# Both heads' masks at the start of a pair of steps: VectorE's order in an attention and mixture-of-experts kernel

## The reference

```python
xn = layernorm(x)                                   # x: 32 samples of 256 rows of 128
# attention: 16 heads of 64, rotary on the first 32 dims of Q and K
scores = where(causal, -inf, einsum('bhqd,bhkd->bhqk', Q, K)) / 8
attn = softmax(scores);  out = einsum('bhqk,bhkd->bhqd', attn, V) @ W_o
# mixture of experts: 8 experts of 128x512 and 512x128, and one "skip" choice
probs = softmax(xn @ router_w + router_b);  gates = the two largest of 9
moe = sum over e of gates[e] * (gelu(xn @ w1[e]) @ w2[e]) + gates[8] * xn
result = x + attention + moe
```

## Time and profile before

| | |
|---|---|
| median of 3 runs | 1558.59 us (1558.15 to 1562.15) |
| the profiled execution | 1554.54 us, span 1552.7 us |
| TensorE, busy share of the span | 81% |
| VectorE | 78% |
| ScalarE | 73% |
| GpSimd | 52% |
| mean granted TensorE clock | 0.947 |

### The profile page before, as it was taken

One profiled execution on the slowest core, in us unless ns is written; L12 is line 12 of the kernel. 1 busy time (PEld: TensorE's weight loads), 2 busy tenths in 40 slices (PEclk: granted clock), 3 DMA queues, 4 the chain that ended last, 5 costly groups with the idle time before them and its releaser, 6 DMA issues.

```text
span 1552.7 us, 47377 instructions
## 1 busy us (share of the span) xinstructions
PE 1263.4 (81%) x15156; PEld 982.4 (63%) x15157; DVE 1213.7 (78%) x4592; ACT 1134.4 (73%) x3606; POOL 806.5 (52%) x1324
## 2 busy tenths in 40 slices
PE   2415888888888888887899999788888888888887
PEld 2403666666666666665798988566666666666666
DVE  6788777777778777775677777788888888887885
ACT  6415777777777777776588887777877777777776
POOL 3243666666666666665000000466766766666665
PEclk9757999999999999999899999999999999999999
DMA  9522322222222222224122322333333333333330
GB/s 296 183 52 52 79 73 70 71 69 69 70 71 69 70 71 70 69 71 133 52 84 85 88 83 79 77 77 78 76 79 76 86 91 83 81 90 95 79 76 26
DMA packets 115839, 130.19 MB, mean 84 GB/s; under 512 B 11568, under 2 KB 75312, under 8 KB 115376
## 3 DMA queue, kind: packets, MB, share of 16 engines
q1 hardware_dynamic: 107056, 110.26, 28.2%
q0 software_dynamic: 8576, 17.33, 3.9%
HBM read 28.85 MB, written 31.59 MB: 39 GB/s over the span
## 4 chain that ended last, share of the span: by engine, by line
PE 42%; DVE 26%; issue 8%; DMA 5%; POOL 4%; ACT 2%; DVEq 0%; POOLq 0%; ACTq 0%
PE bank L1118 8%; DVE arena L972 8%; PE bank L1189 7%; PE bank L1119 7%; PE bank L1120 7%; DVE arena L934 5%; DMA stage<-sorted_y_dram,rows_at 4%; PE bank L1225 4%; PE bank L1199 4%; DVE arena L945 3%; DVE o_whole L1005 2%; DVE arena L933 2%; PE bank L1209 2%; PE bank L1226 1%; DVE stage L891 1%
## 5 line engine op out<-in xcount | busy, mean ns | idle before, releaser
L643 ACT ACTIVATE probs<-arena,neg_max 128x128 f32<-128x128 f32 (+1 forms) x1024 | 453.3, 446 | 109.6 <-DVE neg_max L972 102.5
L972 DVE CUSTOM_DVE_ANT_0 arena<-bank,causal 128x128 f32<-128x128 f32 (+1 forms) x1024 | 314.8, 344 | 2.7 <-PE bank L1189 2.7
L1189 PE MATMUL bank<-arena 64*128 64x128 f16 (+1 forms) x3072 | 179.4, 252 | 128.8 <-DVE neg_max L972 128.3
L501 POOL DMA_INDIRECT stage<-sorted_y_dram,rows_at x128 | 126.3, 986 | 260.9 <-DMA sorted_y_dram<-stage 238.4
L1199 PE MATMUL bank<-ident,probs 128*128 128x128 f32 x1536 | 241.9, 274 | 5.7 <-ACT probsT L626 5.5
L1189 PEld LDWEIGHTS bank<-arena 64*128 64x128 f16 x3072 | 102.9, 97 | 182.8 <-DVE neg_max L972 128.5
L1199 PEld LDWEIGHTS bank<-ident,probs 128*128 128x128 f32 x1536 | 183.2, 142 | 35.7 <-issue 6.4
L626 ACT ACTIVATE probsT<-bank 128x384 f32<-128x384 f32 x384 | 185.9, 484 | 19.3 <-PE bank L1199 19.2
L643 ACT ACTIVATION_READ_ACCUMULATOR probs<-arena,neg_max 128x1 f32 x1024 | 195.4, 191 | 0.0
L1225 PE MATMUL bank<-probsT,arena 128*64 128x256 f32 x1024 | 187.6, 425 | 0.9 <-ACT probsT L626 0.9
L1118 PE MATMUL bank<-xnT_lo,wqk_hi 128*128 128x256 f16 x512 | 143.4, 280 | 54.9 <-DVE arena L934 50.8
(11 more groups left out here) (155 smaller groups left out, 3430.0 us busy)
## 6 DMA issues: line engine op xcount, KB each, us to landing
arena<-arena SPq DMA_DIRECT2D x256, 256.0 KB, 4.7
arena<-sorted_x_dram SPq DMA_DIRECT2D x72, 128.0 KB, 2.1
sorted_y_dram<-stage SPq DMA_DIRECT2D x72, 128.0 KB, 1.8
sorted_x_dram<-arena SPq DMA_DIRECT2D x3, 2304.0 KB, 16.7
arena<-experts_dram SPq DMA_DIRECT2D x8, 512.0 KB, 5.1
out_dram<-acc SPq DMA_DIRECT2D x32, 128.0 KB
sorted_x_dram<-arena SPq DMA_DIRECT2D x1, 2368.0 KB, 16.2
sorted_x_dram<-stage,rows_at POOLq DMA_INDIRECT x128, 2.3
```

The source lines that it names most:

```text
L501: nc.gpsimd.indirect_dma_start(out=stage[:, k % BACKS, :], out_offset=None, in_=sorted_y[0:ROWS, :], in_offset=bass.IndirectOffsetOnAxis(a ...
L643: last = nc.scalar.activation(probs[:, s % 4, at:at + w], masked[:, s % 4, at:at + w], ACT.Exp, bias=neg_max[:, s % 4, t:t + 1], scale=-1. ...
L972: last = nc.vector.tensor_tensor_reduce(out=masked[:, s % 4, at:at + w], in0=SC[s % 2][:, at:at + w], in1=causal[:, at:at + w], scale=1.0, ...
L1189: last = mm(SC[h][:, at:at + w], q_stack[parity][rows, r, ql, u, qs], k_stack[parity][rows, r, kl, u, 0:w], start=(n == 0), stop=(n == 2))
```

## The change

VectorE's `mask` of one head becomes `masks` of two: at the even step it waits for the scores of the pair and for the exponentials of the heads up to s-3 (a wait that `invert` made before), masks head s and head s+1, and then inverts and splits the inverse. The rest of the even step and the rest of the odd step follow as they were. GpSimd waits for `cleared` before its first sample.

```diff
+            pool.wait_ge(cleared, 16 * 5)
             former_samples(sample)
...
-            def mask(b, s, at_fill):
-
-                if s % 2 == 0:
-                    dve.wait_ge(s_ready, 8 * b + s // 2 + 1)
-                    if not (at_fill and s < INV_LAG):
-
-                        invert(8 * b + (s - INV_LAG) // 2, (s - INV_LAG) % H // 2)
-                for t, (at, w) in enumerate(((0, P), (P, 2 * P))):
-                    last = nc.vector.tensor_tensor_reduce(
-                        out=masked[:, s % 4, at:at + w], in0=SC[s % 2][:, at:at + w], in1=causal[:, at:at + w],
-                        scale=1.0, scalar=MASKED, op0=ALU.add, op1=ALU.min, accum_out=neg_max[:, s % 4, t:t + 1])
-                last.then_inc(s_masked, 1)
-                if s % 2 == 0 and not (at_fill and s < INV_LAG):
+            def masks(b, s, at_fill):
+
+                dve.wait_ge(s_ready, 8 * b + s // 2 + 1)
+                if not (b == 0 and s < 4):
+                    dve.wait_ge(exp_done, 16 * b + s - 2)
+                for i in range(2):
+                    for t, (at, w) in enumerate(((0, P), (P, 2 * P))):
+                        last = nc.vector.tensor_tensor_reduce(
+                            out=masked[:, (s + i) % 4, at:at + w], in0=SC[i][:, at:at + w], in1=causal[:, at:at + w],
+                            scale=1.0, scalar=MASKED, op0=ALU.add, op1=ALU.min, accum_out=neg_max[:, (s + i) % 4, t:t + 1])
+                    last.then_inc(s_masked, 1)
+                if not (at_fill and s < INV_LAG):
+                    invert(8 * b + (s - INV_LAG) // 2, (s - INV_LAG) % H // 2)
                     split_inverse(8 * b + (s - INV_LAG) // 2, (s - INV_LAG) % H // 2)
...
             def sample(b, parity, at):
                 for s in range(H):
                     G = 16 * b + s
-                    mask(b, s, at in FILLS)
+                    if s % 2 == 0:
+                        masks(b, s, at in FILLS)
```

## The result

The changed kernel is slower. Its median over 4 runs is 1584.97 us (1569.44 to 1590.52), that of the kernel before beside it 1558.37 us: a ratio of 1.0146, 95% interval 1.01 to 1.0192. The forecast was 1530.6 us and a range of 1516 to 1560.

What follows compares the result with a forecast made beforehand. Waits, not a busy engine, were taken to bound the kernel, chiefly TensorE's scores waiting for mask maxima. First half -36, second half +9, odd samples -1 gave -28 us: 1526.5 profiled, 1530.6 us median, range 1516 to 1560.

Steps and rivals of the forecast that it cites:

- The loop of steps 2 to 8: Masks through turn, rope unit and transposes to next masks: 4.68 us a pair, 5.16 at step 4; no gain against now.
- The scores' wait: TensorE's scores waiting for the masks' maxima, 55.6 us in the first half, would fall to near zero.
- the rope unit's: TensorE's rope unit waiting for the turn: from 21.2 us in the first half to some 45.
- the attention product waits: On TensorE, a wait for the scaled output would appear, about 1 us per sample.
- GpSimd's wait for the clearing: Counted at nothing: it stands where GpSimd idles 25.67 us for the dispatch in any case.
- The rival of the clock that still falls: Gaps of 1.3 and 1.0 us around step 8 still lower the clock: 1545.6 us; chance 0.09.
- the masks of step 2 follow at once, as the scores no longer wait: First half: step 2's masks start when VectorE ends the pair of step 0, at 390.34.
- the term of 1.4 us: First half: step 10's attention product starts at 409.2 instead of 410.63, 1.4 us gained per sample.
- The 1.0 of the clock: First half, behind step 8's gap: the clock stays high, so about 1.0 us per sample comes back.
- the price of the second half: Later masks of step 10 delay gathers and a combine: +0.6 us per sample, +9 us over 15 samples.
- the rival of the gathers: Gathers become the second half's wait: 2.5 us lost per sample instead of 0.6, 1559 us; chance 0.12.
- The contention with GpSimd: VectorE's cast of the inverse waits for GpSimd's subtraction, 0.4 us four times a sample: 1579 us; chance 0.08.

Runs made afterwards that it cites:

- e5_mix_late: `e4_split_first` with VectorE's mix of the former sample moved from step 0 to step 10 in the first half: 1551.37 us, ratio 0.9942 to the kernel before.
- e7_no_clear_wait: The changed kernel without GpSimd's wait for the cleared rows: 1581.94 us, ratio 1.0161 to the kernel before.
- e4_split_first: The changed kernel with GpSimd's waits moved behind its split and rope addition, just ahead of the send or gather needing them: 1562.43 us, ratio 0.9984.
- e6_combine_behind: The changed kernel with the combines of steps 9, 11 and 13 moved one step on, behind the next masks: 1557.64 us, ratio 0.9996.
- e3_turn_ahead: The changed kernel with the odd mask directly behind the turn and the inversion ahead of the even mask: 1576.08 us, ratio 1.0094.
- e10_turn_three: The odd mask directly behind the turn, inversion ahead of the even mask, plus the edits of `e4_split_first`, `e5_mix_late` and `e6_combine_behind`: 1505.28 us, ratio 0.9657.

## Why the prediction was wrong

**What held.** The loop of steps 2 to 8 has the links that the forecast gave it: in the table 4.94, 5.42 and 4.79 for 4.68, 5.16 and 4.68, and in `e5_mix_late`, where nothing else disturbs it, 4.89, 5.22 and 4.75. The scores' wait went, the rope unit's rose to 46.1 and 44.9 us (some 45 forecast), the attention product waits 0.9 us a sample (about 1 forecast), and in the first half the gap of 2.90 us and the low clock behind it are gone: the granted clock of these 14 samples rose from 0.96 to 1.00. The four matmuls of step 10's attention product in sample 7 now take 0.66 us, not 1.13. That the change gains little or nothing in the loop was forecast too. GpSimd's wait for the clearing costs nothing that the runs can tell (`e7_no_clear_wait`). The rival of the clock that still falls is out for this profile.

**The first step that failed: "the masks of step 2 follow at once, as the scores no longer wait".** In sample 7 they come 0.90 us later than that (5.84 for 4.94). The forecast took VectorE's rows at the earlier trace rows as if their lengths and the supply of scores stayed the same. The forecast looked at what TensorE's scores had waited for, and not at what else they depend on once that wait is gone: the chain from a send that lands late, through GpSimd's split, ScalarE's copy and eviction, to the attention product. Of this, `e4_split_first` gives back 0.78 from step 0 to 2; the mix's slowness then costs it again, and only `e5_mix_late` has both off, at 4.07. In addition the links in sample 7 made 0.49 more than forecast over steps 2 to 8 (396.46, 401.80 and 406.55 for the later masks, so 15.01 for 14.52) and the last 0.05. Together 1.44: the attention product of step 10 starts 25.20 us after the sample's first scores (410.90 less 385.70), where it was 25.23 before (410.63 less 385.40) and 23.8 by the forecast. So the term of 1.4 us came out as nothing. The 1.0 of the clock came nearly whole: from that product to the next sample it was 12.47 and is 11.66, so 0.81.

**The second step that failed: the price of the second half, "+0.6 per sample", with ends of 0 and 1.3.** The mechanism was the right one, and the combines' delay was held to be one, at step 13. In the trace two combines wait, 1.72 us at step 9 and 2.23 at step 13, each directly ahead of a pair of masks, and what stands behind is not only the scores, but the exponentials and an eviction on which the next sample's start depends. The masks of step 2 in sample 20 start 5.30 us after the sample's first scores (1117.05 less 1111.75), where the forecast left them at 4.69 (1119.45 less 1114.76). `e6_combine_behind` takes 1.17 of the 1.32 away. The forecast followed the delay of the gathers as far as the next scores, and put it at 0.6; what it left out was what hangs on the exponentials and the eviction. This is the rival of the gathers in kind, given a chance of 0.12, at about half of its price (1.32 a sample against 2.5; the forecast itself had 0.6 of it).

**The rival that was put aside with a row.** The contention with GpSimd was given 0.08, for the four casts of the inverse, and for the two-input instruction it was held that the row of the low part at 406.84 does not show it. That reading was wrong: GpSimd was at work beside that row, and paid. Its first addition began 0.24 us behind the low part:

```profile
407.08 1.03 POOL L470 TENSOR_TENSOR arena<-arena 128x256 f32<-128x256 f32 x1 [0.87 <-DVE arena L934]
408.08 0.71 POOL L471 TENSOR_TENSOR arena<-arena 128x256 f32<-128x256 f32 x1
```

In the kernel before, 91 of the 128 first additions overlap a low part, and take 1.03 us on average; the other 37 take 0.73. The second addition bears on the gap of 2.90 us. The dispatch beside it (407.77) takes 1.10 us for two instructions, and the same two at step 0 take 0.59:

```profile
388.00 0.59 DVE L891 TENSOR_SCALAR stage<-acc,neg_mean,rstd 128x128 f32<-128x128 f32 x2
```

So some 0.5 us of that gap was contention already. In the changed kernel the mix is what suffers (12.9 us, and 8.4 in `e5_mix_late`, over 14 samples: 0.3 each, on the path at step 0), and in the second half the combine, which reads two SBUF tiles (6.9 us more over 14 samples; how much of it is on the path was not tried). In `e3_turn_ahead` it is the low part. The casts of the inverse went the other way, from 0.237 to 0.216 us (first half) and from 0.202 to 0.176 (second) on average of 112. So the mechanism was real and the place wrong.

**The sum.** By the profiled executions: first half -10.8 for 14 samples (forecast -33.6), second half +18.5 (forecast +8.4), and the rest +7.3 (forecast about -1, with the samples 15 and 31 each carrying a share of the halves' figures). In this rest are 2.1 us in sample 0, 2.8 in sample 15 with the experts, 3.1 in the last sample, 1.2 ahead of the first scores, and -1.8 in sample 16. These were not looked into.

**Open.** The median of the changed kernel lies 15.5 us above its profiled execution, that of the kernel before 3.8 above its own. Its runs spread from 1569 to 1591, at clocks of 0.970 to 0.957, and which samples are longer in the long ones no profile shows. The profile of `e7_no_clear_wait` (1576.23 us) has both halves longer by 0.2 a sample at the same mean clock of 0.970, so it is not the clock alone. The low clock in the opening and in the experts was not examined either.

## What to carry to other kernels

When a wait is taken away, follow back each thing that the freed instruction depends on, not only the one it was waiting for: the next latest may be a few tenths of a microsecond behind, and here it was a split on GpSimd that stood behind a transfer's landing. Put waits for transfers just ahead of the instruction that needs them, and not ahead of work that other engines wait for; that is what `e4_split_first` and `e6_combine_behind` changed, and the new order paid only with them and the moved mix. Before a large reordering, try the smallest one: here, with the three moves in place, the odd mask ahead of the dispatch and the combine alone was worth 37 us, and the change 15.6. And when work is moved on VectorE, look at what GpSimd does at the new time, because a row from the old time doesn't give its duration at the new one; and look at GpSimd's own durations, where the cost may stand instead.

## What the runs showed of the hardware

A two-input VectorE instruction on 128x512 took 0.69 us where GpSimd did nothing beside it, and 2.22 us beside two GpSimd instructions of 0.74 and 0.73 us. Which engine pays follows in most rows from which began first. In the kernel before, VectorE began 0.24 us ahead: it took 0.68 us, and GpSimd's addition 1.03 for 0.73. In `e10_turn_three` GpSimd's first addition began ahead as a rule, mostly by 0.32 us, and both additions ran beside the low part in 93 places: the low part took 0.97 us on average, and the second addition, which began within it, 1.16 for 0.72. The 2.22 us do not fit this: VectorE began 0.24 us ahead of the addition there too, but while GpSimd's indexed send before it was still running; why it waited is open. In the trace the lost time is counted as busy and not as idle, so it shows in no list of waits, only in a duration and in the busy time of the stretch. The mix, on 128x128 with one input tile, had 0.34 us an instruction in `e5_mix_late`, and 1.23 us for two beside GpSimd's split; it has one tile as input, so whether it is the other case that the Trainium skill names (GPSIMD Engine Reference, section Specifications), a two-port mode, was not tried.

The gathers that landed late stood beside the stacking transfers: the gather of the combine at step 9 of sample 20 landed 4.6 us after its issue, against 2.5 at the fastest. Of the 32 gathers of the changed kernel whose landing the trace gives, the 15 that overlap a stacking transfer took 4.2 us on average and the other 17 took 3.1. That these transfers are the cause was not tried by itself.
